# A decoder layer on one core: the context turned by VectorE from 128-byte pieces, and new orders for all five engines

## The reference

```python
x = layernorm(x + attention(x))          # linear attention with a memory, head width 128; the running sum is over tokens
x = layernorm(x + long_conv(ctx, x))     # below
x = layernorm(x + ffn(x))                # 4-bit weights with group scales, silu(gate) * up, down, RMS norm

# long_conv: k = v = ctx, q = x, 32 heads of 8 rows, length 512; the layer feeds (B, 256, 512) as (B, H*8, L)
kv  = einsum('bhil,bhjl->bijhl', k, v)                        # products of pairs of rows
y   = irfft(rfft(kv, 1024) * rfft(ssm_kernel, 1024))[..., :512]   # causal convolution along L
out = einsum('bijhl,bhil->bjhl', y + kv * D, q)
```

## Time and profile before

| | |
|---|---|
| median of the runs | 536.75 us |
| span of the profiled execution | 535.3 us |
| TensorE (PE) busy | 508.7 us, 95% |
| VectorE (DVE) busy | 374.4 us, 70% |
| ScalarE (ACT) busy | 415.7 us, 78% |
| GpSimd (POOL) busy | 394.7 us, 74% |
| DMA packets | 66146, of them 37882 under 512 bytes |

### The profile page before, as it was taken

How to read it: one execution, slowest core, us unless ns; L and a number is a source line. 1 busy time by engine, 2 the same in 40 slices (tenths; PEclk the granted TensorE clock), 3 DMA queues, 4 the chain that set the end, 5 groups by cost and what they waited for, 6 DMA issues and landing times.

```text
span 535.3 us, 11768 instructions
## 1 busy us (share of the span) xinstructions
PE 508.7 (95%) x3676; PEld 377.6 (71%) x3676; DVE 374.4 (70%) x1145; ACT 415.7 (78%) x994; POOL 394.7 (74%) x449
## 2 busy tenths in 40 slices
PE   8888899998999999999999999999999999999992
PEld 5676787777785777677767776777677767765660
DVE  2886668988787667776777776768777777763223
ACT  4577875277999788788888897889788877788981
POOL 2768864994898499769968995899589859871231
PEclk9999999999999999999999999999999999999997
DMA  8713776443250862032104210411040111001001
GB/s 224 203 39 63 169 142 180 128 80 99 87 112 24 159 127 86 23 100 79 60 1 117 59 59 0 118 59 59 13 130 14 39 33 49 0 1 42 1 21 39
DMA packets 66146, 40.63 MB, mean 76 GB/s; under 512 B 37882, under 2 KB 55418, under 8 KB 66106
## 3 DMA queue, kind: packets, MB, share of 16 engines
q1 hardware_dynamic: 66106, 40.13, 29.6%
HBM read 27.46 MB, written 12.66 MB: 75 GB/s over the span
## 4 chain that ended last, share of the span: by engine, by line
PE 36%; POOL 27%; issue 19%; ACT 5%; DVE 4%; SPq 4%; DMA 2%; POOLq 1%; DVEq 0%; ACTq 0%
POOL shared L297 9%; POOL h_lo L1102 5%; SPq L415 4%; POOL kv L197 3%; PE p_cv L137 3%; PE p_cv L139 3%; PE p_cv L138 3%; PE p_n L1299 3%; PE p_n L1297 3%; PE p_n L1298 3%; POOL shared L299 2%; PE p_x L1284 2%; PE p_x L1286 2%; PE p_qk L1284 2%; PE p_qk L1286 2%
## 5 line engine op out<-in xcount | busy, mean ns | idle before, releaser
L1102 POOL TENSOR_TENSOR h_lo<-w,h_hi 128x256 f16<-128x256 f32 x88 | 73.6, 842 | 44.6 <-ACT h_hi L1151 43.0
L137 PE MATMUL p_cv<-kv_hi,toe 128*128 128x288 f16 x320 | 91.6, 286 | 1.3 <-DVE shared L257 1.3
L139 PE MATMUL p_cv<-kv_hi,toe 128*128 128x288 f16 x320 | 91.5, 286 | 0.0
L138 PE MATMUL p_cv<-kv_lo,toe 128*128 128x288 f16 x320 | 91.5, 286 | 0.0
L1134 ACT ACTIVATE p_qk<-p_qk,rescale 128x256 f32<-128x256 f32 x192 | 78.3, 451 | 12.5 <-PE p_qk L1286 11.9
L297 POOL TENSOR_TENSOR shared<-shared 128x1024 f32<-128x1024 f32 x32 | 76.8, 2399 | 8.9 <-DVE shared L257 8.8
L1134 ACT ACTIVATE p_x<-p_x,rescale 128x256 f32<-128x256 f32 x192 | 78.4, 452 | 6.2 <-PE p_x L1286 6.0
L1134 ACT ACTIVATE p_s<-p_s,rescale 128x256 f32<-128x256 f32 x144 | 59.0, 456 | 11.2 <-PE p_s L1286 11.1
L1297 PE MATMUL p_n<-wd_hi,h_hi 128*128 128x512 f16 x176 | 66.8, 379 | 0.0
L1298 PE MATMUL p_n<-wd_lo,h_hi 128*128 128x512 f16 x176 | 66.7, 379 | 0.0
L1299 PE MATMUL p_n<-wd_hi,h_lo 128*128 128x512 f16 x176 | 66.7, 379 | 0.0
(11 more groups left out here) (170 smaller groups left out, 1270.6 us busy)
## 6 DMA issues: line engine op xcount, KB each, us to landing
toe<-toeplitz_rows SPq DMA_DIRECT2D x16, 512.0 KB, 4.0
cnat<-in_ctx SPq DMA_DIRECT2D x16, 256.0 KB
xq<-x_blocks SPq DMA_DIRECT2D x16, 256.0 KB, 5.7
xr<-x_rows SPq DMA_DIRECT2D x16, 256.0 KB
out_x<-fin SPq DMA_DIRECT2D x16, 256.0 KB
ring<-in_x SPq DMA_DIRECT2D x6, 512.0 KB, 4.4
x_rows<-ring SPq DMA_DIRECT2D x6, 512.0 KB, 2.9
x_blocks<-ring SPq DMA_DIRECT2D x48, 64.0 KB
```

Source lines behind the costliest of these rows:

```text
L137: nc.tensor.matmul(dst, hi, kh, start=(mb == 0), stop=False)
L138: nc.tensor.matmul(dst, hi, kl, start=False, stop=False)
L139: done = nc.tensor.matmul(dst, lo, kh, start=False, stop=(mb == lb))
L1102: nc.gpsimd.tensor_tensor(h_lo[:, i, :], h32[:, i % 2, :], h_hi[:, i, :], ALU.subtract).then_inc(h_low, 1)
```

## The change

The context no longer passes through ScalarE and TensorE. It is loaded in 128-byte pieces so that each 32x32 block lies where VectorE can transpose it, and VectorE reads the blocks back to front while it transposes them:

```diff
-        self.cnat = [sb(f"cnat{p}", [P, D], F32) for p in range(2)]
-        self.crev = sb("crev", [P, D], F32)
-        self.kT = [sb(f"kT{p}", [P, 2 * LB * 64], F32) for p in range(2)]
+        self.cnat = sb("cnat", [P, B, KD, 32], F32)
+        self.kT = sb("kT", [P, HG * 256], F32)
...
-    def flip_ctx(g, p):          (TensorE; its steps f0 to f3, ct0, ct1 go)
-    def keep_kT(g, p):           (ScalarE; its steps kt go)
-    def reverse_ctx(g, p):       (ScalarE; its steps rv go)
...
 def pair_products(cv, engine, ops, g, h):
-    K = cv.kT[h // 2][:, 256 * (h % 2):256 * (h % 2) + 256]
-    engine.wait_ge(cv.kT_kept, g * 2 + h // 2 + 1)
+    K = cv.kT[:, 256 * h:256 * h + 256]
+    engine.wait_ge(cv.kT_kept, g * 2 + 2)
...
+    def turn_k(g, p):            (VectorE; steps kt0 to kt3, +kt0, +kt1, kt0, kt1)
+        dve.wait_ge(cv.in_ctx[p], (g + 1) * 128)
+        wait(dve, cv.kv_made, g * HG)
+        c = cv.cnat[:]
+        turned = bass.AP(c.tensor, c.offset + 64 * p + 31, [list(c.ap[0]), [32, 2], [P, B], [-1, 32]])
+        nc.vector.transpose(cv.kT[:].rearrange("p (h r j) -> p r h j", h=HG, j=8)[:, 16 * p:16 * p + 16],
+                            turned).then_inc(cv.kT_kept, 1)
...
-        def load_ctx(g, p):
-            sp.dma_start(cv.cnat[p][:], ctx_in[:, g * 32 + p * 16:g * 32 + p * 16 + 16, :]).then_inc(
-                cv.in_ctx[p], 16)
+        def load_ctx(g, k):
+            c = ctx_in[:, g * 32:g * 32 + 32, :].rearrange("b s (k f c) -> k f s b c", f=4, c=32)
+            for f in range(4):
+                sp.dma_start(cv.cnat[32 * f:32 * f + 32, :, k, :], c[k, 3 - f]).then_inc(cv.in_ctx[k // 2], 16)
...
         def deviations(i):
+            wait(act, deviated, 2 * i)
...
         def add_residual(f, t):
+            wait(dve, fin_made[t], f)
```

All order strings are laid out anew. Of the first stage, SyncE's:

```diff
-    START_SYNC = ("x3 x4 cx2 st0 cx3 tw0 x5 st1 st2 x6 st3 toe0 xq0 xq2 toe1 xq1 x7 cx5 cx4 xr1 xr0 toe2 st4 cx6 xq3 "
-                  "xr2 toe3 xq5 xr3 st5 toe4 xq4 cx7 st6 toe5 st7").split()
+    START_SYNC = ("x4 tw0 cx2 cx3 cx0 cx1 x3 cx4 toe1 st0 x5 st1 st2 x6 st3 xq0 toe0 xr1 cx6 cx7 xq1 xr0 cx5 "
+                  "x7 toe2 xq2 cx8 xr2 cx10 cx11 xq3 cx9 toe3 xq4 xr3 cx14 cx12 toe4 toe5 cx13 st4 cx15 xq5 "
+                  "st5 st7 st6").split()
```

the heads of VectorE's and the middle of TensorE's:

```diff
-    START_DVE = ("ze0 is0 u0 sg0 mk0 ig0 dn0 fs0 o0 u1 sg1 ra0 rb0 bm0 mk1 u2 dn1 bn0 o1 kl0 nb0 sg2 ra1 rb1 bm1 mk2 "
+    START_DVE = ("ze0 is0 u0 sg0 mk0 ig0 dn0 sk0 o0 u1 sg1 ra0 rb0 mk1 bm0 u2 dn1 kt0 o1 fs0 ra1 rb1 bn0 kt1 "
...
-                "Oa4 Ob4 w27 w28 Xa6 V5 w29 S5 w30 Xb6 M5 N5 w31 w32 Q6 c0 c1 c2 c3 c4 f2 T5 Oa5 c5 S6 c6 c7 c8 Ob5 "
-                "f3 c9 Xa7 V6 c10 c11 M6 N6 Xb7 c12 rt0 c13 c14 c15 T6 Q7 Oa6 Ob6 +c0 +c1 rt1 S7 V7 xt0 M7 N7 xt1 "
+                "w23 Q5 T4 w24 w25 Oa4 Ob4 w26 Xa6 w27 S5 w28 V5 w29 w30 M5 N5 Xb6 w31 w32 Q6 c0 T5 c1 c2 c3 "
+                "c4 c5 Oa5 Ob5 Xa7 c6 S6 c7 c8 V6 M6 c9 N6 c10 c11 c12 c13 rt0 c14 T6 c15 Oa6 Ob6 +c0 Xb7 "
```

and of a full period, TensorE's start, VectorE's and GpSimd's:

```diff
-    PE_ORDER = ("y1_0 g0_0 g1_0 y1_1 g0_1 y1_2 ct0 g1_1 g0_2 y1_3 y1_4 g2_0 g0_3 c2 g1_2 g3_0 c3 y1_5 g2_1 g1_3 g3_1 "
+    PE_ORDER = ("y1_0 g0_0 g1_0 g2_0 y1_1 y1_2 y1_3 y1_4 g0_1 g1_1 g2_1 y1_5 y1_6 g0_2 g1_2 c2 g0_3 g2_2 c3 "
...
-    DVE_ORDER = ("tm0 tm1 gu0 lk1 tm2 tm3 gu1 tm4 tm5 gu2 lk2 tm6 tm7 tm8 gu3 tm9 tm10 lk3 tm11 gu4 a1 tm12 gu5 tm13 "
-                 "kq0 tm14 tm15 b1 gu6 gu7 ln kq1 bs0 bn0 bs1 bn1 gu8 nm0 gu9 nm1 gu10 xt0 xt1 a0 b0 e1 e0").split()
+    DVE_ORDER = ("tm0 tm1 lk1 gu0 tm2 tm3 gu1 gu2 tm4 tm5 lk2 tm6 tm7 tm8 kt0 gu3 gu4 tm9 tm10 kt1 gu5 lk3 "
+                 "tm11 tm12 tm13 tm14 tm15 a1 kq0 kq1 gu6 gu7 bs0 b1 bn0 ln bs1 gu8 nm0 bn1 gu9 gu10 nm1 xt0 "
+                 "xt1 a0 b0 e0 e1").split()
...
-    POOL_ORDER = ("pr1 hl0 pr2 tr0 hl1 pr3 tr1 hl2 hl3 pn a1 hl4 hl5 tr2 tr3 hl6 bn0 b1 hl7 bn1 hl8 hl9 hl10 a0 b0").split()
+    POOL_ORDER = ("pr1 pr2 hl0 tr0 pr3 hl1 hl2 tr1 hl3 hl4 hl5 pn tr2 a1 tr3 hl6 bn0 hl7 hl8 bn1 hl9 hl10 a0 "
+                  "b1 b0").split()
```

More of the change, by code:

```diff
@@ L155, in flip_x2 @@
         done.then_inc(cv.x2_flipped, 1)
-    return bank_after, flip_ctx, convolve, flip_r, flip_x2
+    return bank_after, convolve, flip_r, flip_x2
 def conv_on_scalar(nc, act, cv):
[L162 to L175, removed]
     def high_kv(g, h):
@@ L286, in low_x2 @@
                                 cv.x2_hi[:, :, c], ALU.subtract).then_inc(cv.x2_low, 1)
-    return low_kv, turn_q, make_terms, sum_x2, statistics_x2, norm_x2, low_x2
+    return low_kv, turn_k, turn_q, make_terms, sum_x2, statistics_x2, norm_x2, low_x2
 def conv_on_pool(nc, pool, cv, halfneg):
@@ L852, in on_tensor @@
     def on_tensor(pe, flips):
-        _, flip_ctx, convolve, flip_r, flip_x2 = flips
+        _, convolve, flip_r, flip_x2 = flips
         def flip(dst, src):
@@ L1075, in body @@
                 if nxt and ctx:
-                    sp.wait_ge(cv.ctx_reversed, it * 2 + 2 + p + 1)
-                    load_ctx(it + 2, p)
+                    sp.wait_ge(cv.kT_kept, it * 2 + 2 + p + 1)
+                    for k in range(2 * p, 2 * p + 2):
+                        load_ctx(it + 2, k)
             if late:
@@ L1374, in decoder_layer @@
-    PE_ORDER = ("y1_0 g0_0 g1_0 y1_1 g0_1 y1_2 ct0 g1_1 g0_2 y1_3 y1_4 g2_0 g0_3 c2 g1_2 g3_0 c3 y1_5 g2_1 g1_3 g3_1 "
[3 rows of a table removed]
-                "y0_8 y0_9 xt1 y0_10").split()
-    DVE_ORDER = ("tm0 tm1 gu0 lk1 tm2 tm3 gu1 tm4 tm5 gu2 lk2 tm6 tm7 tm8 gu3 tm9 tm10 lk3 tm11 gu4 a1 tm12 gu5 tm13 "
-                 "kq0 tm14 tm15 b1 gu6 gu7 ln kq1 bs0 bn0 bs1 bn1 gu8 nm0 gu9 nm1 gu10 xt0 xt1 a0 b0 e1 e0").split()
-    ACT_ORDER = ("rv0 rs0_1 rs1_1 rs0_2 tl rs0_3 rs1_2 gu0 hk1 hh0 rs1_3 rs2_1 rs3_1 rs2_2 gu1 rs3_2 rs2_3 hk2 gu2 hh1 "
-                 "ct0 rs4_1 rv1 rs3_3 rs5_1 rs4_2 rs5_2 gu3 hh2 hk3 rs4_3 rs5_3 rs6_1 n1 hh3 gu4 rs6_2 ho0 gu5 hh4 "
-                 "rs7_1 hh5 kn rs6_3 rs7_2 rs8_1 ct1 rs7_3 rs8_2 gu6 gu7 rs8_3 hh6 rs9_1 rs10_1 rs9_2 ho1 rs10_2 rs9_3 "
-                 "hh7 gu8 rs10_3 gu9 hh8 gu10 hh9 xt0 hh10 xt1 n0").split()
@@ L1385, in decoder_layer @@
-    POOL_ORDER = ("pr1 hl0 pr2 tr0 hl1 pr3 tr1 hl2 hl3 pn a1 hl4 hl5 tr2 tr3 hl6 bn0 b1 hl7 bn1 hl8 hl9 hl10 a0 b0").split()
-    LAST_PE = ("y1_0 y1_1 y1_2 g0_0 g1_0 g2_0 g0_1 g1_1 y1_3 y1_4 g0_2 g2_1 g1_2 y1_5 g0_3 g2_2 g1_3 y1_6 g3_0 g2_3 "
-               "g4_0 g3_1 y1_7 g5_0 y1_8 g4_1 y1_9 g3_2 y0_0 g5_1 g4_2 y1_10 g3_3 g5_2 y0_1 g4_3 y0_2 g6_0 g5_3 g6_1 "
-               "g7_0 y0_3 g6_2 g8_0 g7_1 g6_3 y0_4 g7_2 w1_0 g8_1 g9_0 w1_1 g7_3 y0_5 w1_2 g10_0 g8_2 w1_3 g9_1 "
-               "g10_1 g8_3 g9_2 w1_4 g10_2 w1_5 g9_3 w1_6 g10_3 w1_7 y0_6 w1_8 w1_9 w1_10 y0_7 y0_8 y0_9 y0_10").split()
@@ new lines, in decoder_layer @@
+    START_POOL = ("id0 ms0 ws0 ws1 ws2 ws3 ws4 ws5 ws6 ws7 ws8 ws9 ws10 ws11 ws12 ws13 pw0 ws14 ws15 ws16 "
+                  "ws17 pw1 pw2 pr0 ws18 ws19 ws20 ws21 ws22 ws23 ws24 pw3 ws25 pr1 ws26 ws27 ws28 ws29 ws30 "
+                  "ws31 ws32 pr2 pw4 tr0 pr3 tr1 pr4 tr2 tr3 pq0 pq1 +pr1 +pr2 +tr0 +hl0 +pr3 +hl1 +tr1 +hl2 "
+                  "pw5 +hl3 +pn +tr2 +hl4 +hl5 +tr3 +bn0 +hl6 +hl7 pw6 pw7 +hl8 +bn1 +hl9 +hl10 +a0 +b0").split()
+    PE_ORDER = ("y1_0 g0_0 g1_0 g2_0 y1_1 y1_2 y1_3 y1_4 g0_1 g1_1 g2_1 y1_5 y1_6 g0_2 g1_2 c2 g0_3 g2_2 c3 "
[3 rows of a table added]
+                "g10_3 y0_6 xt0 y0_7 y0_8 d0 y0_9 xt1 y0_10 d1").split()
@@ new lines, in decoder_layer @@
+    DVE_ORDER = ("tm0 tm1 lk1 gu0 tm2 tm3 gu1 gu2 tm4 tm5 lk2 tm6 tm7 tm8 kt0 gu3 gu4 tm9 tm10 kt1 gu5 lk3 "
+                 "tm11 tm12 tm13 tm14 tm15 a1 kq0 kq1 gu6 gu7 bs0 b1 bn0 ln bs1 gu8 nm0 bn1 gu9 gu10 nm1 xt0 "
+                 "xt1 a0 b0 e0 e1").split()
+    ACT_ORDER = ("tl rs0_1 rs1_1 rs2_1 rs0_2 rs1_2 hk1 rs0_3 rs2_2 rs1_3 gu0 rs2_3 hh0 gu1 gu2 rs3_1 hh1 "
+                 "rs4_1 hk2 rs5_1 rs3_2 rs4_2 rs5_2 hh2 rs3_3 rs4_3 rs5_3 gu3 gu4 hh3 hh4 hk3 gu5 ho0 rs6_1 "
+                 "rs7_1 hh5 rs6_2 rs7_2 n1 rs8_1 rs6_3 rs8_2 rs7_3 gu6 gu7 kn rs8_3 hh6 rs9_1 rs10_1 ho1 "
+                 "rs9_2 rs10_2 gu8 rs9_3 rs10_3 hh7 hh8 gu9 gu10 hh9 xt0 hh10 xt1 n0").split()
@@ new lines, in decoder_layer @@
+    POOL_ORDER = ("pr1 pr2 hl0 tr0 pr3 hl1 hl2 tr1 hl3 hl4 hl5 pn tr2 a1 tr3 hl6 bn0 hl7 hl8 bn1 hl9 hl10 a0 "
+                  "b1 b0").split()
+    LAST_PE = ("y1_0 y1_1 g0_0 g1_0 g2_0 y1_2 g0_1 y1_3 g1_1 g2_1 y1_4 g0_2 g1_2 y1_5 g0_3 g2_2 y1_6 g1_3 "
[3 rows of a table added]
+               "w1_10 y0_6 y0_7 y0_8 y0_9 y0_10").split()
+    LAST_DVE = "gu0 gu1 gu2 gu3 gu4 a1 gu5 b1 gu6 gu7 gu8 e1 gu9 gu10 A1 B1 a0 b0 E1 e0".split()
+    LAST_ACT = ("rs0_1 rs1_1 rs2_1 rs0_2 rs1_2 rs2_2 tl rs0_3 rs1_3 gu0 rs2_3 hh0 gu1 gu2 rs3_1 hh1 hh2 "
+                "rs4_1 rs5_1 rs3_2 rs4_2 rs5_2 rs3_3 rs4_3 gu3 rs5_3 gu4 hh3 n1 gu5 rs6_1 rs7_1 hh4 rs8_1 "
+                "rs6_2 rs7_2 rs8_2 rs6_3 rs7_3 hh5 gu6 rs8_3 gu7 ho1 rs9_1 rs10_1 hh6 hh7 rs9_2 rs10_2 rs9_3 "
+                "gu8 rs10_3 hh8 gu9 gu10 hh9 hh10 N1 ho0 n0").split()
@@ L1398, in run @@
```

(3 more changed lines are left out.)

74 lines of the change are left out of this document (26 added, 48 removed), and 51 rows, old and new, of tables (LAST_PE, PE_ORDER, START_ACT, START_DVE).

## The result

| | before | after |
|---|---|---|
| median of the runs | 536.6 us (536.4 to 536.9) | 531.84 us (530.4 to 532.3) |
| span of the profiled execution | 535.3 us | 530.6 us |
| TensorE busy in it | 508.7 us | 504.4 us |
| mean granted clock | 0.995 | 0.988 |

The ratio is 0.990 (95% interval 0.989 to 0.992): faster by 4.8 us. The forecast was 530.0 with a range of 525.5 to 535.5. The profiled execution of the changed kernel is the slowest of its four (532.28; the others 530.42 to 531.88) and has the lowest mean clock (0.988; the others 0.991 to 0.994), so what its trace shows of the start need not hold in full for the others.

The account below looks back on a forecast made before the run. TensorE's time in the loop, and latencies in the start, were taken as the bound. Terms -6.9, -0.8 and +0.9 sum to -6.8: span 528.5, time 530.0 us; own range 527 to 533.5, 8-in-10 range 525.5 to 535.5.

Parts of the forecast that it names:

- Flips, -6.9: Start and periods: 16 groups of four transposes, 0.43 us each, leave TensorE, saving 6.9 us; period 51.20 to 50.3.
- Rival C: Periods 2 to 6: the period doesn't shrink, through the single kept-context buffer or late x2; 534.3 us, chance 0.14.
- Transposes, 0.70 each: VectorE: 16 new 128x512 transposes at 0.70 us (upper bound 1.40), hidden under TensorE in the periods.
- fs0 behind o1, -0.8: Start, VectorE: factor_scales moves behind o1 and sk0 takes its place, shortening the chain by 0.8 us (bounds 0 and -1.5).
- kt0: Start, VectorE's first context transpose: data landed and VectorE ready both at 30.2, so no stall, with no margin.
- Context DMAs, 0.55 each: SyncE: 128 small context loads instead of 16, each costing 0.55 us to issue, between 0.45 and 1.02; hidden in the periods.
- rival B: Start, at kt0 and x7: small context DMAs are dear; 534.7 us at 0.72 each, 543.1 at 1.02; chance 0.12 beyond 0.79.
- Second place, +0.9: Start, 83 to 98 us: later toe0 and x7 loads add 3.0 us, 2.1 absorbed; net +0.9 (bounds -2.1 to +8.6).
- x7 stall (2.8): Start: TensorE wants x7 at 94.4 but its load lands at 97.2, a stall of 2.8 us.
- One sign: Start: TensorE's idle between 20 and 180 us should be near 13, against 11.5 before; far from 13 would count as wrong.
- Ends, 0: Last 60 us: the parts keep their length, ho0 only moving between N1 and n0, so 0 us.
- Steps kept apart, 0: GpSimd's sum and VectorE's low_kv no longer meet: about 1 us per meeting, off TensorE's path in periods, so counted 0.

Follow-up runs that it names:

- path alone: The kernel before with the new context path (128-byte loads, VectorE transposes, no flips or ScalarE copies) and otherwise its old orders: 538.41 us, ratio 1.0025.
- the one with the filler: The changed kernel with twenty unused 512-column matmuls added on TensorE ahead of c0: 531.36 us, ratio 0.990 against the kernel before.
- the single repairs: The changed kernel with toe0 moved far ahead, 530.74 us; separately, with xq1 and x7 right behind toe0, ahead of xr1 and context DMAs, 529.73 us; each ratio 0.987.
- the next one: The changed kernel with toe0 kept behind xq0, and xq1 and x7 issued ahead of xr1 and the context DMAs: 529.73 us, ratio 0.987.

## Why the prediction came out as it did

The ratios add up like this: the new path in the old orders +0.0025 (slower), the new full-period orders on it -0.0059, the last period's orders by themselves -0.0041; -0.0022 is left for the orders of the start, by subtraction (0.0021 either way) and not tested. The path alone gains nothing; the gain shows only with the orders. That the orders of the full periods would do it without the path is unlikely: with 6.9 us of transposes put back on TensorE the changed kernel has a ratio of 1.002. The new period orders with the old path itself were not run.

1. *Flips, -6.9.* They left, and nothing of them is in the trace. TensorE's busy total fell to 504.4 and not to 502; about 2.4 of that is the 4.9 busy us of 90 to 95 at half clock (an estimate). That they "come straight off" where TensorE is full failed. TensorE's steps of one period, each taken against the usual one of its kind (0.12, 0.11, 0.22), hold 0.35 us of gaps before (at `x_lo`) and 0.8 after: 0.45 at `gu6`, and three of 0.08 to 0.13 below the idle column. The period lost 0.46, not 0.86. One of the four is 51.02 us long, with 0.2 us more of such gaps, so they gave 1.6 us of 3.4. Rival C named this outcome (the same period), and with the path alone it is what happens, there through `gu4`'s place behind the transposes. The wait that C had in mind, of the pair product for the transposes, appears when these stand later (1.72). The argument I set against C, GpSimd's 8.3 us of slack, is shown wrong; what C missed is that the new orders win half of it back.
2. *Transposes, 0.70 each.* Right: 0.692 us in the median, the row below. That they are hidden under TensorE was wrong in the path-alone kernel: VectorE had 12.7 us to spare in a period, and still 1.28 us at the wrong place cost TensorE 0.69.
3. *fs0 behind o1, -0.8.* xq0 is issued at 82.54 instead of 83.34, as forecast, but equal orders differed by up to 1.2 us there between executions, so this is not shown. *kt0:* at 29.95 without a wait, forecast 30.2.
4. *Context DMAs, 0.55 each.* 0.49 in the first block (7.86 / 16) and 0.59 in the second (4.69 / 8); rival B falls. The Trainium skill's page "DMA: Bandwidth & Descriptors" (specifications), by which pieces under 512 bytes are read, modified and written, had spoken for B. SyncE's issue doesn't show it. As the cause of toe0's late load it is not shown either: with the same small-piece loads behind it that load landed after 6.9 us in one kernel and after 4.0 in the one with the filler.
5. *Second place, +0.9.* Mis-sized, in the profiled execution. toe0 landed after 6.9 us, not 4.0: `c0` started at 90.09, 3.1 later than the sum has it (87.8, less the 0.8 of fs0 that the sum takes off). Half clock cost 2.1, which I had not thought of. The x7 stall (2.8) was hidden behind these. That makes 2.4 of the 2.9 us by which the start came out worse. The other 0.5 isn't settled; it is the size of the wait before g0_0 that stayed (about 0.5 of 1.40), where I had counted on all of it. One sign agreed by luck: TensorE's idle in 20 to 180 is 13.1 us, as forecast, but with 4.5 for toe0 and nothing for x7.
6. *Ends, 0.* Failed, by 2.1 us: the new last order is worth that by itself. I had compared two moved steps and not followed the rest of the strings. *Steps kept apart, 0:* `low_kv` has a mean of 1477 ns instead of 1642, GpSimd's 512-wide sum of 1371 instead of 1492; what that is worth was not tested by itself.

The new transposes of the changed kernel by line and shape (count, busy us, mean ns). Of the 16 the median is 0.692 us and the longest 2.031; that one alone lifts the mean to 0.771:

```profile
L202 DVE STREAM_TRANSPOSE kT<-cnat 128x512 f32<-128x512 f32 x16 | 12.3, 771 | 0.0
```

Without the 2.1 of the end, which was not in the forecast, the time would have been 533.9 us: the sum was near by luck, for a reason that the working doesn't contain.

## To carry to other kernels

When work leaves an engine that is 99% busy, ask what the rest of its queue would then wait for: the removed work may have been covering a latency, and what replaces it stands in another engine's queue ahead of something. Busy shares give no slack where engines wait for one another: delay one step by a microsecond in thought and follow who waits. Of two waits that are late together, the second shows only when the first is gone, so test them together: here the single repairs gave 1.7 and 1.9 us by their ratios and both gave 4.7. And before a duration of one trace is put down to the order, look for it in a second kernel with the same order: here 6.9 us became 4.0.

## What the runs showed of the hardware

- With TensorE still from 85.6 to 90.1, its granted clock fell to 0.60 and 0.50 (the 1.2 GHz level) and stayed there until 95, five us into renewed work. In the experiment with toe0 early a standstill of 2.9 us was followed by 0.50 from 98 to 101; in the next one 2.8 us were followed by no fall.
- The same load of 512 KB, with the same eight loads of 128-byte pieces issued behind it, landed 6.9 us after its issue in the changed kernel and 4.0 us after it in the one with the filler; the issue alone took SyncE 1.28 us in the first and 0.45 in the second. No run tells why.
- Issuing loads of 256 pieces of 128 bytes cost SyncE 0.49 us each in the first block (7.86 / 16) and 0.75 in the experiment with x7 issued ahead of them (6.00 / 8); single ones in the start of the changed kernel took 0.31 to 1.24.
- A transpose with its input read backwards costs VectorE what a forward one does: medians of 0.692 and 0.697 us in the changed kernel.
